# Two cross-attention layers on one core: GpSimd instead of VectorE spreads two of three sets of softmax reciprocals over their columns

## The reference, cut to what matters

```python
def layer0(x, ctx):                     # 32 query heads of 16, 8 key/value heads
    q, k, v = x @ Wq + bq, ctx @ Wk + bk, ctx @ Wv + bv
    attn = softmax(q k^T / 4 + mask0)   # 32 heads, 100 x 361
    y = (attn v) @ Wo + bo + x
    return layernorm(y) * gamma + beta

def layer1(x, ctx):                     # 16 heads of 32
    a = layernorm(ctx)
    q, k, v = x @ Wq.T, a @ Wk.T, a @ Wv.T
    attn = softmax(where(mask1, q k^T / sqrt(32), -inf))   # 16 heads, 100 x 361
    return x + tanh(gate) * ((attn v) @ Wo.T)

out = layer1(layer0(x, ctx), ctx)
```

## Time and profile before

| | |
|---|---|
| median of 3 runs | 1226.89 us |
| the profiled execution | 1225.93 us |
| its span | 1224.1 us |
| granted TensorE clock, mean | 0.993 |
| busy PE / DVE / ACT / POOL | 93% / 65% / 62% / 21% |
| a batch of the loop | about 72 us |

### The profile page before, as it was taken

One profiled execution on the slowest core, in us unless ns is written; L12 is line 12 of the kernel. 1 busy time (PEld: TensorE's weight loads), 2 busy tenths in 40 slices (PEclk: granted clock), 3 DMA queues, 4 the chain that ended last, 5 costly groups with the idle time before them and its releaser, 6 DMA issues.

```text
span 1224.1 us, 32246 instructions
## 1 busy us (share of the span) xinstructions
PE 1144.3 (93%) x10003; PEld 939.9 (77%) x10003; DVE 800.1 (65%) x2370; ACT 757.7 (62%) x2179; POOL 251.4 (21%) x264
## 2 busy tenths in 40 slices
PE   4899999999999999999999999999999999999997
PEld 4678787786878878687777878778787877878786
DVE  4465667667576675757677675767767576675735
ACT  3464757757475675747567474766747486574744
POOL 1032213111121211113121211312122131211210
PEclk9799999999999999999999999999999999999999
DMA  7774627447362744736365482635647273564500
GB/s 236 196 172 98 162 66 173 109 102 190 76 170 69 158 126 101 190 69 163 85 141 143 89 197 65 170 87 129 153 91 191 60 175 85 124 163 94 142 7 8
DMA packets 77965, 153.77 MB, mean 126 GB/s; under 512 B 10528, under 2 KB 47200, under 8 KB 77296
## 3 DMA queue, kind: packets, MB, share of 16 engines
q1 hardware_dynamic: 77936, 153.40, 51.5%
HBM read 113.72 MB, written 39.65 MB: 125 GB/s over the span
## 4 chain that ended last, share of the span: by engine, by line
PE 75%; issue 10%; ACT 7%; DVE 4%; DMA 1%; DVEq 1%; ACTq 1%; POOL 1%; SPq 0%; POOLq 0%
PE PJ L365 17%; PE TP L416 14%; PE OA L436 6%; PE SCO L402 5%; PE SCO L682 5%; PE SCO L460 5%; PE PJ L468 5%; PE PJ L378 4%; ACT PR L1047 4%; PE SCO L406 4%; PE OA L441 3%; PE SCO L365 2%; DVE SCO L819 2%; ACT PT L1058 1%; PE SCO L667 1%
## 5 line engine op out<-in xcount | busy, mean ns | idle before, releaser
L1047 ACT ACTIVATE PR<-SCO,MN 100x361 f32<-100x361 f32 x768 | 425.9, 566 | 139.8 <-DVE MN L819 138.2
L819 DVE CUSTOM_DVE_ANT_0 SCO<-SCO,MK 100x361 f32<-100x361 f32 x768 | 400.0, 552 | 127.3 <-PE SCO L402 99.1
L416 PEld LDWEIGHTS TP<-ident,PR 100*128 100x128 f32 x2304 | 222.5, 141 | 79.5 <-ACT PT L1058 28.3
L416 PE MATMUL TP<-ident,PR 100*128 100x100 f32 x2304 | 269.9, 253 | 6.7 <-ACT PT L1058 4.4
L1058 ACT ACTIVATE PT<-TP 121x600 f32<-121x600 f32 x256 | 172.0, 672 | 57.3 <-PE TP L416 55.2
L402 PE MATMUL SCO<-K0S,Q0S 128*100 128x362 f32 x512 | 165.4, 374 | 37.6 <-ACT PR L1047 36.0
L1047 ACT ACTIVATION_READ_ACCUMULATOR PR<-SCO,MN 100x1 f32 x768 | 159.5, 208 | 0.0
L829 DVE COPY PT<-TP 121x600 f32<-121x600 f32 x128 | 100.2, 783 | 65.2 <-PE TP L416 61.9
L402 PEld LDWEIGHTS SCO<-K0S,Q0S 128*100 128x100 f32 x512 | 74.7, 166 | 62.4 <-ACT PR L1047 59.7
L819 DVE DVE_READ_ACCUMULATOR2_ANT MN<- 100x1 f32 x768 | 109.2, 142 | 0.0
L1216 POOL TENSOR_TENSOR K1F<-K1F,KB 128x364 f32<-128x364 f32 x64 | 50.7, 792 | 255.9 <-DVE K1F L811 255.9
(11 more groups left out here) (140 smaller groups left out, 1809.7 us busy)
## 6 DMA issues: line engine op xcount, KB each, us to landing
K1S<-k_scr SPq DMA_DIRECT2D x128, 364.0 KB, 6.0
k_scr<-K1HL SPq DMA_DIRECT2D x64, 364.0 KB, 2.6
Q0S<-q_scr SPq DMA_DIRECT2D x128, 100.0 KB, 4.0
K0S<-k_scr SPq DMA_DIRECT2D x64, 182.0 KB, 4.9
AT<-ctx_cols SPq DMA_DIRECT2D x16, 722.0 KB, 9.4
V<-ctx_rows SPq DMA_DIRECT2D x16, 484.0 KB
q_scr<-QHL SPq DMA_DIRECT2D x16, 400.0 KB, 2.5
k_scr<-K1HL SPq DMA_DIRECT2D x32, 182.0 KB, 3.0
```

The lines of the kernel that those rows point to most:

```text
L416: last = pe.transpose(TP[:, k % 2, c * T:(c + 1) * T], PR[0:T, k % NPR, c * SP:c * SP + P], ident[0:T, 0:T])
L819: dve.tensor_tensor_reduce(out=bank, in0=bank, in1=mask[0:T, :], scale=scale, scalar=3.4e38, op0=ALU.add, op1=ALU.min, accum_out=MN[0:T, k ...
L1047: act.activation(PR[0:T, k % NPR, 0:S], SCO[0:T, k % 3, 0:S], ACT.Exp, bias=MN[0:T, k:k + 1], scale=-1.0, accum_out=SM[0:T, k:k + 1]).then ...
```

## The change

DVE keeps the three reciprocals of a batch, and the spreading for u = 1. The spreading for u = 0 and u = 2 goes to POOL. For u = 0 POOL uses two copies of 100x128 (`repeat_sums0`), behind block 3 of the keys; for u = 2 it uses one copy of 100x512 (`repeat_sums2`), at the head of the next batch, ahead of block 2 of the keys. Each waits for the reciprocals (`rcp`) and for the last reader of SX (`attn`).

```diff
-            def repeat_sums(b, u):
+            def reciprocals(b, u):
                 dve.wait_ge(prob, NH * b + 16 * u + 16)
                 wait_from(dve, sums_x, 3 * b + u)
                 dve.reciprocal(RSM[0:T, :], SM[0:T, 16 * u:16 * u + 16]).then_inc(rcp, 1)
-                wait_from(dve, attn, 3 * b + u)
-                dve.wait_ge(rcp, 3 * b + u + 1)
-                sums = RSM[0:T, :]
...
+            def repeat_sums1(b):
+                wait_from(dve, attn, 3 * b + 1)
+                dve.wait_ge(rcp, 3 * b + 2)
...
                     if p == 1 and not first:
-                        repeat_sums(b - 1, 2)
+                        reciprocals(b - 1, 2)
...
                     if p == 9:
-                        repeat_sums(b, 0)
+                        reciprocals(b, 0)
...
-                repeat_sums(b, 1)
+                reciprocals(b, 1)
+                repeat_sums1(b)
...
+            def repeat_sums0(b):
+                wait_from(pool, attn, 3 * b)
+                pool.wait_ge(rcp, 3 * b + 1)
+                src = RSM[0:T, :].rearrange("p (a g j) -> p g j a", a=2, g=2).unsqueeze(4).to_broadcast([T, 2, NJ, 2, HD0])
+                pool.sem_inc(met_pool, 1)
+                for g in range(2):
+                    last = pool.tensor_copy(SX[0:T, g, :].rearrange("p (j a d) -> p j a d", j=NJ, a=2), src[:, g])
+                last.then_inc(sums_x, 1)
+
+            def repeat_sums2(b):
+                pool.wait_ge(attn, 3 * b + 2)
+                pool.wait_ge(rcp, 3 * b + 3)
+                src = RSM[0:T, :].unsqueeze(2).to_broadcast([T, 16, HD1])
+                pool.sem_inc(met_pool, 1)
+                pool.tensor_copy(SX[0:T, :, :].rearrange("p m (j d) -> p (m j) d", j=NJ), src).then_inc(sums_x, 1)
...
-            def batch(b, more):
+            def batch(b, first, more):
+                if not first:
+                    repeat_sums2(b - 1)
                 keys1_low(b, 2)
...
                 keys1_low(b, 3)
+                if first:
+                    pool.wait_ge(rep_id, 1)
+                repeat_sums0(b)
                 pool.wait_ge(l_xn, 16 * b + 16)
...
+            repeat_sums2(NB - 1)
```

More of the change, by code:

```diff
@@ L834, in repeat_sums @@
                 dve.reciprocal(RSM[0:T, :], SM[0:T, 16 * u:16 * u + 16]).then_inc(rcp, 1)
-                wait_from(dve, attn, 3 * b + u)
-                dve.wait_ge(rcp, 3 * b + u + 1)
-                sums = RSM[0:T, :]
[L838 to L844, removed]
+            def repeat_sums1(b):
+                wait_from(dve, attn, 3 * b + 1)
+                dve.wait_ge(rcp, 3 * b + 2)
+                src = RSM[0:T, :].rearrange("p (a g j) -> p g j a", a=2, g=2).unsqueeze(4).to_broadcast([T, 2, NJ, 2, HD0])
+                dve.tensor_copy(SX[0:T, 0:2, :].rearrange("p g (j a d) -> p g j a d", j=NJ, a=2), src)\
+                    .then_inc(sums_x, 1)
             def unit_outputs(b, u):
@@ L1010, in _ @@
             probs_out(NB - 1, NPAIR - 3)
-            repeat_sums(NB - 1, 2)
+            reciprocals(NB - 1, 2)
             probs_out(NB - 1, NPAIR - 1)
@@ L1259, in batch @@
                 pool.tensor_tensor(Y[0:T, :], Y[0:T, :], GB[0:T, :], ALU.add).then_inc(y_b, 1)
-            batch(0, True)
+            batch(0, True, True)
             with pool.Fori(1, NB - 1) as b:
-                batch(b, True)
-            batch(NB - 1, False)
+                batch(b, False, True)
+            batch(NB - 1, False, False)
+            repeat_sums2(NB - 1)
 def kernel(**inputs):
```

## The result

The changed kernel took 1229.59 us in the median of 12 runs (1227.79 to 1231.53) against 1226.96 us for the kernel before in the same job. The ratio is 1.0021, with a 95% interval of 1.0013 to 1.0028: 2.6 us slower, 1.6 to 3.4. The prediction was 1227.5 us and a range of 1225 to 1235, with 0.56 for a change within 0.2% and 0.37 for slower. The measured 0.21% lies on that border.

A forecast was written before the change was run, and what follows sets the result against it. PE holds 75% of the chain that ended last, DVE 4%, POOL 1%. 15 times 0.04 us gives 0.6 us, all else nothing: 1226.5 us against the profiled 1225.93, plus 1.0 for the runs' median, 1227.5 us; range 1225 to 1235.

The forecast's parts named there:

- the forecast's own range: Whole kernel: 1226.0 to 1229.3 us, 0 to 2.4 us more, if the u = 2 copy takes 0.45 to 0.75 us; chance 0.54.
- Nothing gained on DVE: Where DVE drops the u = 2 and u = 0 copies, PE is waited for: gain nothing, at most 0.10 us for u = 2.
- The third rival: DVE was the one waited for at u = 2 and u = 0: 1.5 to 6 us less, 1221 to 1225.4 us; chance 0.09.
- The relay, first arm: POOL's copy delays key block 2's bias, ACT's high part and the exponential: 0.04 us a batch counted (0.07 computed), 0.6 us over 15.
- D: Duration of POOL's 100x512 copy for u = 2, put at 0.66 us between bounds of 0.45 and 1.64 us.
- The second arm: POOL's later second half of block 2 delays DVE's scaling of block 3; PE held 0.32 us, taken up by a later wait.
- PE's later wait: At 573.85, a few instructions behind the held score, PE waited 0.37 us for ACT; predicted to take up the 0.32 us.
- The second rival: PE's wait at 573.85 moves along with the delay: 0.32 us a batch, 4.8 us in all, 1231.7 us; chance 0.13.
- The first rival (a slow copy): POOL copies at its bias rate, 1.11 us: 7.8 us more, 1234.7 us; at the addition's 1.28 us, 1237.3; chance 0.24.
- the break-even: Duration of POOL's u = 2 copy up to which the delayed exponential at the batch head costs nothing: 0.59 us.
- u = 0, u = 1, the ends of the program: POOL's u = 0 copies end 5 us early; u = 1 stays on DVE, serialised with POOL; first and last batch hidden: cost nothing.
- all else nothing: In the sum, everything besides 15 times 0.04 us at the batch head was taken to cost nothing.

The follow-up runs named there:

- Three copies between the halves: Against the changed kernel, the u = 2 copy stands between POOL's two halves of key block 2 and is made three times in a row: 1227.39 us, ratio 1.0001.
- five copies: Against the changed kernel, the u = 2 copy stands between POOL's two halves of key block 2 and is made five times: 1257.46 us, ratio 1.0244.

## Why the prediction was right, and where it was off

The forecast was 0.6 us more, and 2.6 were measured. 1229.59 us lies beyond the forecast's own range (to 1229.3) and within the whole one because that was drawn wide, for two rivals that both turned out false; that the number stayed inside it owes something to luck. What held is the account of who waits for whom.

**Nothing gained on DVE: right, shown.** DVE's copy of probabilities starts at the same distance, and the batch with only u = 0 moved is 72.00 us. The third rival is out at both places in the loop.

**The relay, first arm: right in mechanism and place, its size too small.** The prediction had 0.04 to 0.07 us a batch; it is 0.13 in the changed kernel, 0.16 with only u = 2 moved. Against the sum 566.78 + 0.08 + D + 0.79 + 0.03 + 0.39:

| term | predicted | measured |
|---|---|---|
| reciprocals end to copy start | 0.08 | 0.16 |
| D | 0.66 | 0.61 |
| copy end to bias start | 0 | -0.04 |
| bias | 0.79 | 0.79 |
| bias end to ACT's high part | 0.03 | 0.12 |
| high part to exponential | 0.39 | 0.42 |
| sum, reciprocals' end to exponential | 1.95 | 2.06 |
| the same before the change | 1.88 | 1.88 |
| so the exponential is late by | 0.07 | 0.18 |

The mis-sized terms are the two hand-offs, 0.17 us together more. The last step is 0.03 longer, too; D, predicted 0.05 too long, and the overlap of 0.04 between copy and bias took a part back (the prediction had allowed for 0.03 of overlap, which makes its 0.04 out of 0.07). I had read each hand-off at another instruction than the one that would wait (DVE's scaling to POOL, and ACT's high part of block 3). The rows of the program show a difference for the second: for block 3 the wait for the bias stands on the activation itself, for block 2 on an instruction ahead of it. That this is the reason for 0.12 in place of 0.03 is argued, not shown. For the first I know no reason; all copies behind the reciprocals start so late, those of u = 0 (0.17 us) as well.

**The second arm: right, shown.** DVE's scaling of block 3 waits for POOL (0.94 us; "some 0.9" was predicted), the score of pair 4 is held, and PE's later wait, 0.23 us where it was 0.37, takes it up. Three copies between the halves show it at a delay of 1.01 us, and the four batches at full clock with five copies show it at 2.55. The second rival, with this wait moving along, is out. The sizes were near: both kernels give a slack of 0.69 us (1.01 - 0.32, 2.55 - 1.86) where the prediction had 0.55, and 0.31 us taken up where it had 0.37.

**The first rival (a slow copy)** is out by D = 0.61. The kernel became slower all the same, because the break-even lay at about D = 0.44 (the exponential is 0.17 us late in the mean of the loop at D = 0.61) and not at 0.59.

**u = 0, u = 1, the ends of the program: right in the loop.** The u = 0 copies end 0.52 us after their start, 5.6 us ahead of PE. The prediction also said that moving the contended u = 1 copy would help; with all three on POOL nothing was gained, since DVE isn't waited for there and its stall only passed on.

**The sum.** 15 times 0.135 is 2.0 us of the measured 2.6 (1.6 to 3.4). The rest lies within the interval. Batch 0 holds another 0.2 us (43.19 us from its u = 1 reciprocals to those of u = 2, before 42.99), and the traces of the experiments narrow it down. It arises at one DVE instruction, the small step from the statistics of Y (YVE), which in batch 0 starts 0.53 us behind the one before it and not 0.32. The 0.53 stands in every trace with the u = 0 copies on POOL except that with all three there (0.16); with only u = 2 moved it is 0.32. So the prediction's "all else nothing" missed a term of 0.2 us, paid once. Why the instruction starts later stays open.

## What to carry to other kernels

Work given to an idle engine costs nothing only if the instructions behind it on that engine have slack: look at what the new wait holds up, and put it behind the last step that somebody is waiting for. Here one slot lower in POOL's program made 2 us of loss vanish. When a slack is as small as the sum of a few hand-offs, each of them must be read at the very instruction that will wait; a neighbour's can be off by 0.1 us. And an engine's freed time is worth nothing where it was waiting anyway, nor where the stall only passes to its next instruction.

## What the runs showed of the hardware

- POOL's copy of 512 columns from a source repeated 32 times took 611 ns, of 128 columns 292 ns: if both lie on one line, 0.83 ns a column and 0.19 us that doesn't grow. The 100x512 addition took 1.28 us.
- A POOL copy that waited for the one before it started 0.16 to 0.17 us behind its end.
- A two-input DVE subtraction of 364 columns took 1.94 us beside POOL's subtraction and 0.54 without.
- With five copies between the halves PE was nearly idle for some 1.7 us in each batch. In ten of the 14 batches of the loop the granted clock then fell to 0.5 for about 3 us; in four, with the same wait, it stayed at 1.00. In the profiles of the other nine kernels, where PE's waits in the loop were at most 1.2 us, it stayed at 1.00 all through the loop.
